# Second cross-attention: value and sum products in 512-column blocks, and nine key chunks added up on GpSimd in place of eight

## The reference, cut to what matters

```python
def _L1_xattn_ref(qkv, y):                       # qkv: layernorm(x), y: ctx_2048 (4, 1601, 512)
    N_HEADS = 16
    bs, width, length = qkv.shape
    ch = width // N_HEADS                        # 32
    q = qkv.reshape(bs * N_HEADS, ch, length)
    k = v = y.reshape(bs * N_HEADS, ch, -1)
    scale = 1.0 / math.sqrt(math.sqrt(ch))
    weight = jnp.einsum('bct,bcs->bts', q * scale, k * scale)
    weight = jax.nn.softmax(weight.astype(jnp.float32), axis=-1).astype(weight.dtype)
    a = jnp.einsum('bts,bcs->bct', weight, v)
    return a.reshape(bs, -1, length)

x = x + jnp.tanh(g_xattn[1]) * _L1_xattn_ref(_layernorm(x, axis=-1), ctx_2048)
```

## Time and profile before

| | |
|---|---|
| median of 3 runs | 1889.31 us (1888.81 to 1891.34) |
| the profiled execution | 1887.21 us, its span 1885.4 us |
| second cross-attention | about 787 to 1610 us of the span |
| PE, DVE, ACT, POOL busy, share of the span | 88%, 63%, 46%, 44% |

### The profile page before, as it was taken

One profiled execution on the slowest core, in us unless ns is written; L12 is line 12 of the kernel. 1 busy time (PEld: TensorE's weight loads), 2 busy tenths in 40 slices (PEclk: granted clock), 3 DMA queues, 4 the chain that ended last, 5 costly groups with the idle time before them and its releaser, 6 DMA issues. The chain is left out here.

```text
span 1885.4 us, 26473 instructions
## 1 busy us (share of the span) xinstructions
PE 1664.2 (88%) x9744; PEld 655.1 (35%) x9744; DVE 1187.1 (63%) x1538; ACT 867.2 (46%) x1273; POOL 827.9 (44%) x324
## 2 busy tenths in 40 slices
PE   5999999798666766799999999899999999699898
PEld 2444444344333332122222223223223322344443
DVE  3768999885364445877766766566777640544543
ACT  1221211211655654167777777676767778111111
POOL 0022233543323524367766666576777668100000
PEclk9999999899798988699999999999999999799999
DMA  9232222313353444402222222211222224000000
GB/s 328 76 106 73 81 97 87 103 34 107 135 138 116 134 132 125 97 14 62 64 65 65 65 65 65 66 41 50 53 52 64 65 53 93 1 0 22 22 23 23
DMA packets 141020, 144.32 MB, mean 77 GB/s; under 512 B 60238, under 2 KB 110690, under 8 KB 140902
## 3 DMA queue, kind: packets, MB, share of 16 engines
q1 hardware_dynamic: 128998, 105.99, 21.2%
q10 hardware_dynamic: 11904, 36.74, 5.9%
HBM read 99.73 MB, written 23.88 MB: 66 GB/s over the span
## 5 line engine op out<-in xcount | busy, mean ns | idle before, releaser
L1509 ACT ACTIVATE c_prob<-c_scores,ctx_scales 128x512 f32<-128x512 f32 (+1 forms) x832 | 551.6, 686 | 271.1 <-PE c_scores L1561 219.1
L1425 DVE TENSOR_REDUCE c_piece_max<-c_unit 128x1 f32<-128x804 f32 x512 | 485.3, 984 | 235.4 <-PE c_unit L1544 228.3
L1366 POOL TENSOR_TENSOR c_prob_sum<-c_prob_sum,c_prob 128x2048 f32<-128x2048 f32 x96 | 435.1, 4533 | 16.6 <-ACT c_prob L1509 9.5
L1561 PE MATMUL c_scores<-c_queries,c_keys 97*128 97x512 f16 (+1 forms) x832 | 320.1, 390 | 28.8 <-ACT c_prob L1509 19.0
L1544 PE MATMUL c_unit<-c_khigh,c_qdiag 128*128 128x402 f16 x1024 | 259.2, 348 | 30.2 <-DMA c_qdiag<-c_qhigh 11.2
L1576 PE MATMUL c_out<-c_prob,c_VT 128*32 128x256 f32 (+2 forms) x3200 | 263.0, 401 | 0.0
L676 PE MATMUL a_S<-a_ctxT,a_xnT 128*128 128x401 f32 x512 | 190.4, 516 | 7.2 <-ACT a_prob L633 3.9
L706 PE MATMUL a_o<-a_ctx,a_probT 128*128 128x512 f32 (+1 forms) x416 | 183.4, 598 | 0.0
L1561 PEld LDWEIGHTS c_scores<-c_queries,c_keys 97*128 97x128 f16 (+1 forms) x832 | 80.0, 98 | 268.7 <-issue 141.0
L1366 POOL TENSOR_TENSOR c_prob_sum<-c_prob 128x2048 f32<-128x2048 f32 x16 | 72.6, 4537 | 168.4 <-ACT c_prob L1509 151.2
L1544 PEld LDWEIGHTS c_unit<-c_khigh,c_qdiag 128*128 128x128 f16 x1024 | 78.5, 98 | 174.0 <-DVE c_piece_max L1425 94.9
(11 more groups left out here) (197 smaller groups left out, 1997.5 us busy)
## 6 DMA issues: line engine op xcount, KB each, us to landing
c_keys<-key_parts SPq DMA_DIRECT2D x48, 400.5 KB, 4.2
b_k<-in_keys ACTq DMA_DIRECT2D x16, 801.0 KB, 6.1
a_ctx<-in_ctx SPq DMA_DIRECT2D x12, 1024.0 KB, 5.9
c_VT<-in_values SPq DMA_DIRECT2D x16, 768.0 KB
a_ctxT<-in_ctxT SPq DMA_DIRECT2D x12, 802.0 KB, 4.7
key_parts<-b_khigh ACTq DMA_DIRECT2D x16, 400.5 KB, 2.9
key_parts<-b_krest ACTq DMA_DIRECT2D x16, 400.5 KB, 4.7
c_khigh<-key_parts SPq DMA_DIRECT2D x16, 400.5 KB, 4.0
```

The source lines that it names most:

```text
L1366: nc.gpsimd.tensor_tensor(psum4[:], a[:], prob[(j * MC + c) % RING][:], ALU.add).then_inc(sums_taken, 2 if i == 1 else 1)
L1425: nc.vector.tensor_reduce(piece_max[j % 2][:, k // 2, k % 2:k % 2 + 1], U[bank(unit)][:, :, 0:PIECE], axis=AX.XY, op=ALU.max).then_inc(uni ...
L1509: nc.scalar.activation(prob[(j * MC + c) % RING][0:w, h, :], STp[h % 2][0:w, :], ACT.Exp, scale=score_scale[0:w]).then_inc(exp_done, 1)
L1561: nc.tensor.matmul(STp[h % 2][0:w, :], K[p][:, h, c * P:c * P + w], Q[p][:, h, :], start=True, stop=True).then_inc(scores_ready, 1)
```

## The change

`POOLED` gets chunk 4, so that GpSimd makes 8 additions in a group and SUMMED is 7, 10, 11, 12. All of `out`, `den` and `den_of_sum` become whole blocks of 512 columns with gaps of their own, and the weight of a block in the rule that spreads the units is 1.25.

```diff
-        POOLED = [0, 1, 2, 3, 5, 6, 8, 9]
+        POOLED = [0, 1, 2, 3, 4, 5, 6, 8, 9]
...
                 add_up(g, j, 7)
+                add_up(g, j, 8)
...
-            def den_of_sum(g, half):
-                cols = columns(half)
-                if half == 0:
-                    pe.wait_ge(sums_taken, (g + 1) * NP)
+            def den_of_sum(g):
+                pe.wait_ge(sums_taken, (g + 1) * NP)
                 for h in range(H):
-                    last = nc.tensor.matmul(DEN[h * CH:(h + 1) * CH, cols], ones32[:], psum4[:, h, cols], start=False, stop=half == 1)
-                if half == 1:
-                    last.then_inc(den_done, 1)
+                    last = nc.tensor.matmul(DEN[h * CH:(h + 1) * CH, :], ones32[:], psum4[:, h, :], start=False, stop=True)
+                last.then_inc(den_done, 1)
...
             def placed(before):
 
                 gaps = {}
-                for c in range(1, MC):
-                    for b in {1: [], 2: [0], 3: [1, 2]}.get(c, [c - 1]):
-                        at = 4 * c + (1 if b == c - 1 else 0)
-                        if b == 0:
-                            gaps.setdefault(at + 1, []).append(("out", b, WHOLE))
-                            continue
-                        gaps.setdefault(at, []).append(("out", b, 0))
-                        gaps.setdefault(at + (2 if b not in SUMMED else 1), []).append(("out", b, 1))
-                        if b == SUMMED[0]:
-                            gaps.setdefault(at + 2, []).append(("den", b, WHOLE))
-                        elif b in SUMMED:
-                            gaps.setdefault(at + 2, []).append(("den", b, 0))
-                            gaps.setdefault(at + 3, []).append(("den", b, 1))
-                for half in range(2):
-                    gaps.setdefault(4 * MC + 1 + half, []).append(("out", MC - 1, half))
+                for c in range(1, MC + 1):
+                    for i, b in enumerate({1: [], 2: [0], 3: [1, 2]}.get(c, [c - 1])):
+                        gaps[4 * c + 1 + 2 * i] = ("out", b)
+                        if b in SUMMED and b < MC - 1:
+                            gaps[4 * c + 3] = ("den", b)
                 if before:
-                    for i in range(4):
-                        gaps.setdefault(4 + i, []).append(("last", None, i))
+                    gaps[5], gaps[7] = ("last den", None), ("den of sum", None)
                 return gaps
...
-                HALF, PAIR = 0.53, 0.36
-                weights = {gap: sum(HALF * (1 + (what != "last" and half == WHOLE)) for what, b, half in parts) for gap, parts in gaps.items()}
-                per_gap = (sum(weights.values()) + PAIR * max(len(stream), UNITS)) / (H * MC)
+                BLOCK, PAIR = 1.25, 0.36
+                per_gap = (BLOCK * len(gaps) + PAIR * max(len(stream), UNITS)) / (H * MC)
```

More of the change, by code:

```diff
@@ L1561, in score, with out @@
                 nc.tensor.matmul(STp[h % 2][0:w, :], K[p][:, h, c * P:c * P + w], Q[p][:, h, :], start=True, stop=True).then_inc(scores_ready, 1)
[L1563 to L1569, removed]
+            def out(g, j, c):
+                w = P if c < MC - 1 else ML
                 if c == 0:
@@ L1572, in out, with den @@
                     wait(pe, out_taken, g)
-                if half != 1:
-                    pe.wait_ge(exp_done, EXPS0 + g * EXPS + H * (c + 1))
+                pe.wait_ge(exp_done, EXPS0 + g * EXPS + H * (c + 1))
                 for h in range(H):
[L1576 to L1585, removed]
+                    last = nc.tensor.matmul(O[h * CH:(h + 1) * CH, :], VT[j % 2][0:w, c, h * CH:(h + 1) * CH],
+                                            prob[(j * MC + c) % RING][0:w, h, :], start=c == 0, stop=c == MC - 1)
+                if c == MC - 1:
+                    last.then_inc(out_done, 1)
+                elif c not in SUMMED:
+                    last.then_inc(pv_done, 1)
+            def den(g, j, c):
+                w = P if c < MC - 1 else ML
                 if c == SUMMED[0]:
@@ L1588, in den @@
                 for h in range(H):
-                    last = nc.tensor.matmul(DEN[h * CH:(h + 1) * CH, cols], ones32[0:w, :], prob[(j * MC + c) % RING][0:w, h, cols],
+                    last = nc.tensor.matmul(DEN[h * CH:(h + 1) * CH, :], ones32[0:w, :], prob[(j * MC + c) % RING][0:w, h, :],
                                             start=c == SUMMED[0], stop=False)
-                if half > 0:
-                    last.then_inc(pv_done, 1)
-            def den_of_sum(g, half):
-                cols = columns(half)
-                if half == 0:
-                    pe.wait_ge(sums_taken, (g + 1) * NP)
-                for h in range(H):
-                    last = nc.tensor.matmul(DEN[h * CH:(h + 1) * CH, cols], ones32[:], psum4[:, h, cols], start=False, stop=half == 1)
-                if half == 1:
-                    last.then_inc(den_done, 1)
@@ L1603, in last_sums @@
[L1603 to L1607, removed]
+                last.then_inc(pv_done, 1)
+            def den_of_sum(g):
+                pe.wait_ge(sums_taken, (g + 1) * NP)
+                for h in range(H):
+                    last = nc.tensor.matmul(DEN[h * CH:(h + 1) * CH, :], ones32[:], psum4[:, h, :], start=False, stop=True)
+                last.then_inc(den_done, 1)
@@ L1649, in products @@
                     nonlocal given, done
[L1650 to L1657, removed]
+                    what, b = gaps.get(gap, (None, None))
+                    if what == "out":
+                        out(g, j, b)
+                    elif what == "den":
+                        den(g, j, b)
+                    elif what == "last den":
+                        den(g - 1, (j - 1) % TURN, MC - 1)
+                    elif what == "den of sum":
+                        den_of_sum(g - 1)
+                    if what:
+                        done += BLOCK
                     upto = (gap - 3) * per_gap
@@ L1675, in slot @@
                 if not nxt:
-                    for i in range(4):
-                        last_sums(g, j, i)
+                    den(g, j, MC - 1)
+                    den_of_sum(g)
                 assert given == len(stream), (given, len(stream))
```

## The result

| | before | changed |
|---|---|---|
| median | 1889.27 us (4 runs) | 1983.78 us (4 runs, 1980.69 to 1988.68) |
| ratio, 95% interval | | 1.050 (1.0476 to 1.0525) |
| profiled execution | 1887.21 us, span 1885.4 | 1985.32 us, span 1983.5 |

Predicted were 1975 us and a range of 1925 to 2005. The span grew by 98.1 us, all of it in the second cross-attention.

What follows compares the result with a forecast made beforehand. A chain through GpSimd that touches ACT, 51.07 us a group, was taken as the bound. +77 us for groups and ends and +9 for the clock, +86 on the profiled 1887.2, gave 1973, as a median 1975 us; range 1925 to 2005.

Steps and rivals of the forecast that it cites:

- Part (a): From a group's first addition to `add_gain` on GpSimd: later reciprocals make it 10.45 us in place of 8.71.
- the chain: GpSimd's additions and ACT's exponentials, from one group's first addition to the next's: 51.07 us, said to set the group's length.
- Part (c): From exponential e(7,0) to e(10,0): three chunks each wait for an addition, 14.04 us in place of 10.62, plus 3.4.
- (b): From `add_gain` to exponential e(7,0): 11.98 us, predicted to stay.
- Part (d): From exponential e(10,0) to the next group's first addition: 19.8 us against 19.76 before, bounds 16.6 and 20.7.
- clumps: Units close together behind `rows` and around score e(1',0), DVE taking 0.93 us each: PE stands still 2.0 and 1.2 us.
- The rival in which the clumps cost nothing: Units close together do not hold PE up: +1.9 us a group, 1931 us in all, chance 0.15.
- The sum without the clock: +5.1 us for each of 14 steps from group 1 to group 15, 71; with both ends +77.
- The first period: Group 0, which has no `add_gain` and 16 units more: +2 us, between 0 and 5.
- What follows the last first addition: At the end, one addition more (4.53 us) less two joined blocks: +4 us.
- The clock: PE's granted clock falling after waits: a third of 1.7 us in each of 16 groups, +9, between 0 and 27.
- PE's lighter work: In each group PE saves 2.7 us by joining halves, 1.0 by chunk 4's block, 1.5 by empty gaps: 5.2 us.

Runs made afterwards that it cites:

- e3_gain_late: The changed kernel with `add_gain` moved from behind a group's first addition to behind the addition of chunk 6: 1944.58 us, ratio 1.029.
- e1_whole_eight: The changed kernel with chunk 4 taken out of GpSimd's additions again (eight pooled chunks), whole blocks and weight 1.25 kept: 1945.78 us, ratio 1.029.
- e4_weight_half: The changed kernel with a block's weight in the rule that spreads the units 0.5 in place of 1.25: 1909.12 us, ratio 1.009.
- e6_best_guess: The changed kernel with eight pooled chunks (chunk 4 on PE), a block's weight 0.3 and `add_gain` behind the addition of chunk 5: 1836.91 us, ratio 0.972.
- e8_halves_spread: The kernel before (halves, eight pooled chunks) with `add_gain` behind the addition of chunk 5 and a half's weight 0.15 for 0.53: 1863.71 us, ratio 0.986.
- e7_before_gain_late: The kernel before with `add_gain` moved behind the addition of chunk 5, nothing else: 1886.80 us, ratio 0.998.
- e2_halves_nine: The kernel before with chunk 4 added up on GpSimd (nine pooled chunks), products still in halves with the old weights: 1979.03 us, ratio 1.047.

## Why the prediction was right, point by point

**Part (a) longer by 1.7.** Measured 8.71 to 10.38. The first reciprocal was to start 4.30 us behind the first addition and the fourth at 9.4; DVE's timeline has them at 4.23 and 9.36:

```profile
1028.03 0.95 DVE L1445 RECIPROCAL c_rden<-c_den 128x128 f32<-128x128 f32 x1
...
1033.16 0.94 DVE L1445 RECIPROCAL c_rden<-c_den 128x128 f32<-128x128 f32 x1
```

e3_gain_late shows that the wait for the reciprocals lay in the chain.

**Part (c) longer by 3.4.** Measured: (b) and (c) together went from 22.60 to 26.00, as predicted, (b) 11.95 and (c) 14.05 of it, and each of e(6,0) to e(10,0) was released by GpSimd. e1_whole_eight shows that without the ninth chunk these waits are gone.

**Part (d) unchanged.** 20.16 us in the group of the loop without a fall of the clock, where 19.76 were measured before and 19.8 predicted. That the saved PE work is eaten by clumps is borne out by PE's 104 us of waiting for DVE and by e4_weight_half. The rival in which the clumps cost nothing was to give 1931 us, and is excluded.

**The sum without the clock.** A written-out group went from 50.7 to 55.9, 5.2 us more, and one of the loop from 51.05 to 56.54, 5.5 more, where 5.1 were predicted. The first period was 2.3 longer (57.25 to 59.56; predicted 2). What follows the last first addition grew by 5.9 us (316.7 to 322.6; predicted 4).

**The clock** is the term that was mis-sized. I took a third of 1.7 us in each of 16 groups, 9 us. In the trace of the changed kernel the clock fell behind the clump at `rows` in eight of the 13 middle groups, and each of these falls cost part (d) 21.73 - 20.16 = 1.57 us, 12.6 us in all. A fall costs nearly the full 1.7 there because it comes where PE sets the pace; "a third, since PE has slack elsewhere" was the wrong step for this place. For other places it was right: a fall at 860.9, in part (a) of a group, cost nothing (55.93 against 55.90), and one at 1588.0 cost 0.3. The last period grew by 8.6 us, 3.4 more than the chain's 5.2, with three falls in it where there was one before; I take that for the clock too, which isn't shown. So the clock cost about 16 us, 7 more than predicted.

**The rest of the miss.** The profiled execution took 1985 us where 1973 were predicted, the medians are 1984 and 1975. Of the 12 us, 7 are the clock's, 3 come from the chain's growth in 14 groups, and 2 from what follows the last first addition.

**PE's lighter work, 5.2 us in a group,** wasn't seen in the changed kernel but is real. e6_best_guess against e8_halves_spread puts whole blocks at 2.0 us in a group, where 17 x 0.16 = 2.7 for joining and 1.5 for empty gaps were counted. Some of the rest may be taken by PE's waits for DVE, 33.5 us in all in e6_best_guess against 8.9 in e8_halves_spread. No run tests this.

**What I had too strong** is "a group lasts as long as this chain". It was so, but PE's side was as long, as e7_before_gain_late shows. For a change that lengthens the chain this made no difference. For the move that shortens it, the gain was 0.2 us in a group and not the 1 to 3 that the chain alone allowed.

## What to carry to other kernels

Before work is moved to an engine with much idle time, look at what its results release: GpSimd had 15 us free in each group of 51 and the added 4.5 us still went into the time, because its additions started late, behind `add_gain`, and then gave ring buffers back at one per 4.68 us while the producer wanted one per 3.5. An in-order engine that idles in the middle of such a chain (here for reciprocals needed only by `add_gain`) should do that waiting behind the work that releases others. And when block sizes change, the rule that spreads other work among them has to be set anew and by trial: its one weight moved the time by 75 us with nine chunks and by 103 with eight.

## What the runs showed of the hardware

The granted clock fell to 1.2 GHz in the changed kernel at the same place of the group in eight of 13 groups, behind four waits of PE of 0.17 to 0.62 us within 3.5 us in which it was busy for 2.19 us. A wait of 1.47 us for ACT stands ahead of them and had ended about 5 us before the fall. In neighbouring groups with the same instructions and waits it did not fall (910.40 to 966.30, clock 1.00), so that two lengths of the same group stand in one trace.

The clump alone did not bring the falls at `rows` about. e1_whole_eight has no such fall and e3_gain_late one, both with the same short waits but without the wait of 1.5 us for ACT ahead of them. e2_halves_nine, where PE waits less for DVE (35.0 us) and more for ACT (75.6), has a fall in ten of its 13 middle groups. So these falls went with the ring's waits on top of PE's other ones; how the two share the cause is not shown.

Single long waits are not needed. In the kernel before, PE ran units alone ahead of the first group, one per 0.90 us with a wait of 0.39 us at each, and the clock fell there too. Two of PE's rows, and windows before and after the fall:

```profile
768.30 0.52 PE L1544 MATMUL c_unit<-c_khigh,c_qdiag 128*128 128x402 f16 x2 [0.39 <-DVE c_piece_max L1425]
769.21 0.70 PE L1544 MATMUL c_unit<-c_khigh,c_qdiag 128*128 128x402 f16 x2 [0.39 <-DVE c_piece_max L1425]
```

```profile
core 0: us, PE busy (x) PEld busy (x) DVE busy (x) ACT busy (x) POOL busy (x), PEclk, DMA share, GB/s
766.00:769.40 3.40, 1.85 (x9) 0.45 (x8) 3.40 (x5) 0.00 (x0) 3.34 (x2) 1.00 0.00 0
769.40:772.80 3.40, 2.96 (x8) 0.39 (x6) 3.35 (x4) 0.00 (x0) 3.40 (x1) 0.50 0.00 0
```

The prediction looked at the fall in group 14 only, behind a wait of 1.27 us, and could have seen this one.

A block of four 32-column products with 256 columns takes 0.58 us and one with 512 takes 1.00, and in the changed kernel a whole block takes 0.99 (from 1011.36 to the next score at 1012.35). The Trainium skill (Perfetto Trace Analysis, Matmuls) states that larger matmuls are more efficient. The traces agree, at 27 us for the kernel, once the chain and the clumps are out of the way.
